# A gated cross-attention block with top-2 experts on one core: routing products in the tokens' layout, b2's products in one contraction, block-diagonal values laid out contiguously

## The reference

```python
x = x + tanh(g_xattn) * attn(layernorm(x), ctx, ctx, mask, Wq, Wk, Wv, Wo, 16)
x = x + tanh(g_ffn) * ffn(layernorm(x), Wg, bg, W1, b1, W2, b2)

# attn: 16 heads of 64
scores = einsum('bhqd,bhkd->bhqk', qh, kh) + attn_mask
ctx = einsum('bhqk,bhkd->bhqd', softmax(scores), vh)        # then Wo

# ffn: 8 experts, hidden width 256
probs = softmax(xf @ Wg + bg)
w, idx = top_k(probs, 2);  w = w / sum(w)
comb = sum(one_hot(idx, 8) * w[..., None], axis=1)
h = relu(einsum('nd,edh->enh', xf, W1) + b1[:, None, :])
y = einsum('enh,ehd->end', h, W2) + b2[:, None, :]
out = einsum('end,ne->nd', y, comb)
```

## Time and profile before

| | us |
|---|---|
| median of 3 runs | 1108.44 (1108.04 to 1109.18) |
| the profiled execution, its own time | 1107.66 |
| its span | 1105.6 |
| PE busy | 1024.9 (93%) |
| ACT busy | 943.1 (85%) |
| DVE busy | 894.4 (81%) |
| POOL busy | 791.7 (72%) |

### The profile page before, as it was taken

One profiled execution on the slowest core, in us unless ns is written; L12 is line 12 of the kernel. 1 busy time (PEld: TensorE's weight loads), 2 busy tenths in 40 slices (PEclk: granted clock), 3 DMA queues, 4 the chain that ended last, 5 costly groups with the idle time before them and its releaser, 6 DMA issues.

```text
span 1105.6 us, 36301 instructions
## 1 busy us (share of the span) xinstructions
PE 1024.9 (93%) x13797; PEld 755.4 (68%) x13797; DVE 894.4 (81%) x1803; ACT 943.1 (85%) x1809; POOL 791.7 (72%) x719
## 2 busy tenths in 40 slices
PE   5868799999999999999999999999999999999887
PEld 4446567776777777677777767777776777777655
DVE  2686688897888889788888978888897888787766
ACT  3988788889898888989888898988889898887865
POOL 3566667776867777686777768777776877788843
PEclk9999899999999999999999999999999999999999
DMA  9122121212112121211212121121212111111100
GB/s 219 33 56 59 49 56 43 55 45 59 50 40 57 52 57 43 59 50 40 57 52 56 43 59 50 40 57 52 54 45 59 50 31 46 44 40 50 29 3 20
DMA packets 123162, 56.90 MB, mean 51 GB/s; under 512 B 26584, under 2 KB 122864, under 8 KB 122992
## 3 DMA queue, kind: packets, MB, share of 16 engines
q1 hardware_dynamic: 122992, 54.59, 19.3%
HBM read 16.80 MB, written 4.19 MB: 19 GB/s over the span
## 4 chain that ended last, share of the span: by engine, by line
PE 49%; DVE 14%; ACT 12%; issue 12%; POOL 11%; DMA 1%; ACTq 0%; DVEq 0%; SPq 0%; POOLq 0%
PE bank L44 15%; PE bank L46 14%; PE bank L45 14%; POOL hidL L895 3%; POOL ptL L932 3%; ACT qH L464 3%; POOL rstd L880 3%; PE bank L307 2%; ACT bank L520 2%; PE bank L262 2%; DVE shift L668 2%; ACT x2hat L508 1%; DVE comb L868 1%; ACT vH L559 1%; DVE above L844 1%
## 5 line engine op out<-in xcount | busy, mean ns | idle before, releaser
L895 POOL TENSOR_TENSOR hidL<-hid,hidH 128x512 f16<-128x512 f32 x242 | 278.6, 1164 | 21.3 <-ACT hidH L494 21.3
L932 POOL TENSOR_TENSOR ptL<-pt,ptH 128x512 f16<-128x512 f32 x128 | 148.5, 1160 | 179.4 <-ACT pt L579 179.4
L675 DVE TENSOR_TENSOR qL<-bank,qH 128x512 f16<-128x512 f32 x224 | 153.4, 685 | 57.1 <-ACT qH L464 53.7
L484 ACT ACTIVATE hid<-bank,b1col 128x512 f32<-128x512 f32 x256 | 185.6, 725 | 8.3 <-PE bank L46 8.2
L494 ACT ACTIVATE hidH<-bank,b1col 128x512 f16<-128x512 f32 x256 | 188.3, 736 | 0.0
L464 ACT ACTIVATE qH<-bank 128x512 f16<-128x512 f32 x256 | 155.1, 609 | 36.0 <-PE bank L46 35.0
L44 PE MATMUL bank<-w2H,hidH 128*128 128x128 f16 x1024 | 179.0, 220 | 5.8 <-DVE hidL L788 5.2
L46 PE MATMUL bank<-w2H,hidL 128*128 128x128 f16 x1024 | 179.1, 220 | 0.0
L45 PE MATMUL bank<-w2L,hidH 128*128 128x128 f16 x1024 | 179.1, 220 | 0.0
L927 POOL TENSOR_TENSOR x<-x,y_scaled 128x512 f32<-128x512 f32 x114 | 146.0, 1280 | 14.1 <-DVE x L746 14.1
L938 POOL TENSOR_TENSOR prob<-prob,row_inv 128x512 f32<-128x512 f32 x128 | 133.4, 1043 | 15.2 <-DVE row_inv L782 15.2
(11 more groups left out here) (143 smaller groups left out, 3607.3 us busy)
## 6 DMA issues: line engine op xcount, KB each, us to landing
vdH<-vH SPq DMA_DIRECT2D x256, 64.0 KB, 2.1
vdL<-vL SPq DMA_DIRECT2D x256, 64.0 KB, 2.1
x_raw<-in_x SPq DMA_DIRECT2D x16, 256.0 KB, 3.0
ctx_raw<-in_ctx SPq DMA_DIRECT2D x16, 256.0 KB, 3.1
mask_raw<-in_fside_Bx1xSxS SPq DMA_DIRECT2D x32, 128.0 KB, 2.8
out_x<-x SPq DMA_DIRECT2D x16, 256.0 KB, 2.5
qH<-in_L_xattn_Wq SPq DMA_DIRECT2D x1, 512.0 KB, 6.0
qH<-in_L_xattn_Wk SPq DMA_DIRECT2D x1, 512.0 KB, 8.1
```

What stands on the lines that cost most here:

```text
L484: act.activation(hid[:, k % NR, :], bk("hid", g, e, c)[:, :], ACT.Relu, bias=b1col[:, e, c:c + 1]).then_inc(s_relu[c], 1)
L675: dve.tensor_tensor(qL[at], bk("Q", g, h)[:, :].rearrange("p (b q) -> p b q", b=GB), qH[at], ALU.subtract).then_inc(s_q_low[h % 2], 1)
L895: pool.tensor_tensor(hidL[:, m % 2, c, :], hid[:, k % NR, :], hidH[:, m % 2, c, :], ALU.subtract).then_inc(s_hid_low[c], 1)
L932: pool.tensor_tensor(ptL[:, b % 2, :], pt[:, b % 2, :], ptH[:, b % 2, :], ALU.subtract).then_inc(s_pt_low, 1)
```

## The change

Three edits.

1. The layouts of `wv`, `v` and `vd` have the chunk outside and the 64 head dimensions innermost. The 128 weights of a product lie next to each other. A placement transfer moves eight runs of 64 elements (128 B) per partition. The split of Wv at the start writes its low half in two instructions instead of one, per bank.
2. The logits are made with tokens on the partitions: the transposed activations are stationary (128 columns), `wgH`/`wgL` with 8 columns move, three passes for each of four tiles, at `i` = 0. `logitT`, `logit_t` and their transposes go, with one turn of the banks. The scale 1/32 moves into DVE's addition of the bias.
3. The three products of b2 are stacked on the partitions in blocks of 32 (`QUAD`): the weights of the picked experts are written three times (`weight3`), one transpose brings the three copies to partitions 0, 32 and 64, ACT writes all of them rounded to fp16, and DVE replaces the third by its low half. b2 is loaded three times, and its second copy replaced by its low half. One matmul per tile over 96 partitions gives the sum of the three products. The unused rows are zeroed by POOL at the start.

```diff
-CL = 4
+CW = 4
 HC = HID // P
 WS = 32.0
+QUAD = 32
+STACK = 3 * QUAD
...
-        wvH, wvL = (sb(f"wv{p}", [P, 2, C // CL, DV, CL], F16) for p in "HL")
+        wvH, wvL = (sb(f"wv{p}", [P, 2, C, DV], F16) for p in "HL")
...
-        b2H, b2L = (sb(f"b2{p}", [E, D], F16) for p in "HL")
+        b2_halves = sb("b2_halves", [STACK, D], F16)
...
-        vH, vL = (sb(f"v{p}", [P, 2, C // CL, DV, CL], F16) for p in "HL")
-        vdH, vdL = (sb(f"vd{p}", [P, 2, 2, C // CL, 2, DV, CL], F16) for p in "HL")
+        vH, vL = (sb(f"v{p}", [P, 2, C, DV], F16) for p in "HL")
+        vdH, vdL = (sb(f"vd{p}", [P, 2, 2, C, 2, DV], F16) for p in "HL")
         otH, otL = (sb(f"ot{p}", [P, 2, C, 2, S], F16) for p in "HL")
 
-        logit_t = sb("logit_t", [E, N])
...
+        weight3 = sb("weight3", [P, GT, 3, QUAD])
...
-        pickedT_H, pickedT_L = (sb(f"pickedT_{p}", [E, N], F16) for p in "HL")
+        pickedT = sb("pickedT", [STACK, N], F16)
...
-                    lhs = [v[:, t % 2, b % 2, c // CL, :, :, c % CL].rearrange("p g d -> p (g d)") for v in (vdH, vdL)]
+                    lhs = [v[:, t % 2, b % 2, c, :, :].rearrange("p g d -> p (g d)") for v in (vdH, vdL)]
...
-                if i == 7 and within(g - 1, GROUPS):
-                    for freed in take_bank("logitT", g - 1):
-                        pe.wait_ge(*freed)
-                    pe.wait_ge(s_x2T_low, g)
-                    three_passes(pe, bk("logitT", g - 1)[0:E, :], (wgH[:, :], wgL[:, :]),
-                                 (x2tH[:, (g - 1) % 2, :], x2tL[:, (g - 1) % 2, :])).then_inc(s_logitT, 1)
                 if i == 0 and within(g - 2, GROUPS):
                     for freed in take_bank("logit", g - 2):
                         pe.wait_ge(*freed)
-                    pe.wait_ge(s_logitT_out, g - 1)
+                    pe.wait_ge(s_x2T_low, g - 1)
                     for t in range(GT):
-                        last = pe.transpose(bk("logit", g - 2)[:, t * E:(t + 1) * E], logit_t[:, t * P:(t + 1) * P],
-                                            ident[0:E, 0:E])
+                        lhs = [c[:, g % 2, t * P:(t + 1) * P] for c in (x2tH, x2tL)]
+                        last = three_passes(pe, bk("logit", g - 2)[:, t * E:(t + 1) * E], lhs, (wgH[:, :], wgL[:, :]))
                     last.then_inc(s_logit, 1)
                 if i == 2 and within(g - 2, GROUPS):
                     for freed in take_bank("pickedT", g - 2):
                         pe.wait_ge(*freed)
                     pe.wait_ge(s_comb1, g - 1)
                     for t in range(GT):
-                        last = pe.transpose(bk("pickedT", g - 2)[0:E, t * P:(t + 1) * P], picked[:, t, :], ident[:, :])
+                        last = pe.transpose(bk("pickedT", g - 2)[0:STACK, t * P:(t + 1) * P],
+                                            weight3[:, t, :, :].rearrange("p n e -> p (n e)"), ident[:, :])
                     last.then_inc(s_pickT, 1)
                 if i == 3 and within(g - 2, GROUPS):
                     for freed in take_bank("b2 out", g - 2):
@@ -445,8 +442,8 @@
                     pe.wait_ge(s_pickT_low, g - 1)
                     for t in range(GT):
                         cols = slice(t * P, (t + 1) * P)
-                        last = three_passes(pe, bk("b2 out", g - 2)[:, t * D:(t + 1) * D],
-                                            (pickedT_H[:, cols], pickedT_L[:, cols]), (b2H[:, :], b2L[:, :]))
+                        last = pe.matmul(bk("b2 out", g - 2)[:, t * D:(t + 1) * D], pickedT[:, cols], b2_halves[:, :],
+                                         start=True, stop=True)
                     last.then_inc(s_b2, 1)
...
-            act.wait_ge(s_load["b2"], 16)
-            act.activation(b2H[:, :], b2_raw, ACT.Copy, scale=WS).then_inc(s_wact, 1)
+            act.wait_ge(s_load["b2"], 16 * 3)
+            act.activation(b2_halves[:, :], b2_raw, ACT.Copy, scale=WS).then_inc(s_wact, 1)
...
-                if i == 7 and within(g - 1, GROUPS):
-                    act.wait_ge(s_logitT, g)
-                    if g >= 2:
-                        act.wait_ge(s_logit, g - 1)
-                    act.activation(logit_t[:, :], bk("logitT", g - 1)[0:E, :], ACT.Copy,
-                                   scale=1.0 / WS).then_inc(s_logitT_out, 1)
...
-                weights_low(H // 4 + n, wvL[:, :, n, :, :],
-                            bk("weights", H // 4 + n)[:, :].rearrange("p (c g d) -> p g d c", c=CL, g=2), wvH[:, :, n, :, :])
+                dve.wait_ge(s_wact, H // 4 + n + 1)
+                some = slice(CW * n, CW * (n + 1))
+                for g2 in range(2):
+                    last = dve.scalar_tensor_tensor(
+                        wvL[:, g2, some, :], bk("weights", H // 4 + n)[:, :].rearrange("p (c g d) -> p g c d", c=CW, g=2)[:, g2],
+                        WS, wvH[:, g2, some, :], ALU.mult, ALU.subtract)
+                last.then_inc(s_wdve, 1)
...
-            weights_low(H // 4 + 5, b2L[:, :], b2_raw, b2H[:, :])
+            weights_low(H // 4 + 5, b2_halves[QUAD:QUAD + E, :], b2_raw[QUAD:QUAD + E], b2_halves[QUAD:QUAD + E, :])
...
-                    dve.tensor_tensor(l, bk("logit", g - 2)[:, 0:GT * E].rearrange("p (t e) -> p t e", t=GT),
-                                      bgrow[:, :].unsqueeze(1).to_broadcast([P, GT, E]), ALU.add).then_inc(s_logit_in, 1)
+                    dve.scalar_tensor_tensor(l, bk("logit", g - 2)[:, 0:GT * E].rearrange("p (t e) -> p t e", t=GT),
+                                             1.0 / WS, bgrow[:, :].unsqueeze(1).to_broadcast([P, GT, E]), ALU.mult,
+                                             ALU.add).then_inc(s_logit_in, 1)
...
-                    dve.tensor_tensor(picked[:, :, :], picked[:, :, :],
-                                      picked_inv[:, :].unsqueeze(2).to_broadcast([P, GT, E]), ALU.mult).then_inc(s_comb1, 1)
+                    if g == 2:
+                        dve.wait_ge(s_w3zero, 1)
+                    dve.tensor_tensor(weight3[:, :, :, 0:E], picked[:, :, :].unsqueeze(2).to_broadcast([P, GT, 3, E]),
+                                      picked_inv[:, :].unsqueeze(2).unsqueeze(3).to_broadcast([P, GT, 3, E]),
+                                      ALU.mult).then_inc(s_comb1, 1)
                     dve.wait_ge(s_comb1, g - 1)
                     if g >= 4:
                         dve.wait_ge(s_scaled, E * (g - 3))
-                    dve.tensor_scalar(comb[:, g % 2], picked[:, :, :], out_scale[:, 1:2], None, ALU.mult).then_inc(s_comb, 1)
+                    dve.tensor_scalar(comb[:, g % 2], weight3[:, :, 0, 0:E], out_scale[:, 1:2], None,
+                                      ALU.mult).then_inc(s_comb, 1)
                 if i == 2 and within(g - 2, GROUPS):
                     dve.wait_ge(s_pickT_high, g - 1)
-                    dve.scalar_tensor_tensor(pickedT_L[:, :], bk("pickedT", g - 2)[0:E, :], WS, pickedT_H[:, :], ALU.mult,
-                                             ALU.subtract).then_inc(s_pickT_low, 1)
+                    third = slice(2 * QUAD, 2 * QUAD + E)
+                    dve.scalar_tensor_tensor(pickedT[third, :], bk("pickedT", g - 2)[third, :], WS, pickedT[third, :],
+                                             ALU.mult, ALU.subtract).then_inc(s_pickT_low, 1)
...
-            pool.memset(vdH[:, :, :, :, :, :, :], 0.0).then_inc(s_vzero, 1)
-            pool.memset(vdL[:, :, :, :, :, :, :], 0.0).then_inc(s_vzero, 1)
+            pool.memset(b2_raw, 0.0).then_inc(s_b2zero, 1)
+            pool.memset(weight3[:, :, :, :], 0.0).then_inc(s_w3zero, 1)
+            pool.memset(vdH[:, :, :, :, :, :], 0.0).then_inc(s_vzero, 1)
+            pool.memset(vdL[:, :, :, :, :, :], 0.0).then_inc(s_vzero, 1)
...
-            load("b2", b2_raw, b2)
+            sp.wait_ge(s_b2zero, 1)
+            for n in range(3):
+                load("b2", b2_raw[n * QUAD:n * QUAD + E], b2)
...
-                            sp.dma_start(dst[g2 * S:(g2 + 1) * S, t % 2, b2_, :, g2].rearrange("p a d c -> p a (d c)"),
-                                         src[b2_ * S:(b2_ + 1) * S, g2].rearrange("p a d c -> p a (d c)")
-                                         ).then_inc(s_place[t % 2][g2], 16)
+                            sp.dma_start(dst[g2 * S:(g2 + 1) * S, t % 2, b2_, :, g2, :],
+                                         src[b2_ * S:(b2_ + 1) * S, g2]).then_inc(s_place[t % 2][g2], 16)
```

More of the change, by code:

```diff
@@ L126, in flamingo_block @@
         wg_raw = q_bytes[1][:, 2176:2176 + E]
-        b2_raw = q_bytes[1][0:E, 2304:2304 + D]
+        b2_raw = q_bytes[1][0:STACK, 2304:2304 + D]
         w1_raw = [as_f32(h[:, :, :, :], "p a c n -> p (a c n)") for h in (hidH, hidL)]
@@ L147, in flamingo_block @@
         s_q, s_v, s_scores, s_pt, s_pv, s_wo = (sem(n) for n in ("q", "v", "scores", "pt", "pv", "wo"))
-        s_hid, s_y, s_logitT, s_logit, s_pickT, s_b2 = (
-            sem(n) for n in ("hid", "y", "logitT", "logit", "pickedT", "b2out"))
```

(27 more changed lines are left out.)

## The result

The changed kernel takes 1081.91 us (1080.65 to 1082.70) against 1108.81 us, 0.9757 of the time with a 95% interval of 0.9740 to 0.9774: 26.9 us faster. The forecast was 1084.7, which is 23.7 us faster by its sum, in a range of 1077 to 1097. The profiled execution took 1082.21 us, its span 1080.4.

What follows compares the result with a forecast made beforehand. PE's issue spacing was taken as the bound. Savings of 1.57 us per group over 13.5 groups (21.2), plus 3.0 at the ramps, less 0.5 at the start, gave 23.7 us: 1084.7 us, range 1077 to 1097.

Steps and rivals of the forecast that it cites:

- What bounds the kernel: Steady part: PE issues almost without a hole and sets the pace, busy 62.45 of 64.70 us per group.
- Part 1: Value blocks: contiguous vd loads at 98 ns, not 117, saving 0.097 us per block, 12.4 us of PE time.
- Part 2: Routing products at steps 7 and 0: net 0.73 us of PE time saved per group, 11.7 us for 16.
- Part 3: b2's block: twelve matmuls become four, saving 0.45 us per group, 7.2 us in all; no price for height.
- Part 4: Placement DMAs: 128 B packets at 18 ns, 2.3 us per step, hidden behind 12 us of slack.
- rival 4: Placement DMAs: a 128 B write costs 57 ns, twice a 512 B packet, and DMA sets the pace; 1133, chance 0.08.
- What reaches the end: Of 1.96 us saved per group, 1.57 counts: routing, b2 and four value blocks; the rest falls into PE's waits.
- groups of 63.1 us: Steady part: the length of a group of eight steps expected in the profile after, where it was 64.7 us.
- The start's loss of 0.5 us: Kernel start: POOL memsets, two more b2 loads and split wvL subtractions, counted as 0.5 us lost.
- Rival 2: Steady part: other engines take over, ACT bounds more than two stretches per group, half the gain goes; 1096, chance 0.12.

Runs made afterwards that it cites:

- e3: The kernel before with b2's stacked product alone: 1098.66 us, ratio 0.9914.
- e2: The kernel before with the routing products in the tokens' layout alone: 1096.12 us, ratio 0.9892.
- e5: The kernel before with value chunks interleaved by two in place of four, vd's weights two elements apart: 1103.80 us, ratio 0.9954.
- e6: The kernel before with value chunks interleaved by eight in place of four, vd's weights eight elements apart: 1149.90 us, ratio 1.0367.
- e10: The changed kernel with each of b2's four 96-row matmuls issued three times into the same place, twelve as before: 1088.87 us.
- e1: The kernel before with the contiguous value layout and its 128 B placement runs alone: 1104.04 us, ratio 0.9962.
- e8: The changed kernel with DVE's residual ahead of y_scaled in even steps and the second layernorm's variance and root a step earlier: 1046.91 us, ratio 0.9450.

## Why the prediction was right

**What bounds the kernel.** Right: PE's spacing. What shortened it in an open stretch arrived: 0.60 of b2's 0.64 us per group (e3), and all of what was removed at step 7 (e2).

**Part 1.** Right in cause and size: 98 ns, 0.70 us. e5 and e6 settle the cause: of what the value block reads only the step changed, and the loads followed. The Trainium skill, page Advanced Engine Details and Errata, section SBUF Cachelines, asks for two hits on a 16-byte line; at 8 bytes there are two, and the load still takes 117 ns. One hit (16 bytes) is far worse, 167 ns, and four hits are free. So the rule gives the direction and is a factor of two too generous here.

**Part 2.** The mechanism was right, the term mis-sized: 0.95 us per group where I had 0.73. I had the matmuls at 29 ns (25 measured) and kept b2's handovers of 0.15 us (0.06 measured). Those belonged to the small tile (shown for b2 by e10) and went with it.

**Part 3.** Right in mechanism, mis-sized for the same reason: 0.64 in place of 0.45 (e10).

**Part 4.** Right: hidden. I took 18 ns per packet, 11 were measured, and the DMA share became 27% in a group and not near 40. The Trainium skill, page DMA: Bandwidth & Descriptors, section Specifications, has a read-modify-write below 512 B. Whether it takes place no row shows; a packet of 128 B took 11 ns against 28 for 512 B, dearer by the byte but far from the 57 ns of rival 4.

**What reaches the end.** Here two errors of opposite sign met, so that the forecast came as near as 3 us is in part luck. The sizes were too small: 37.8 us on PE, not 31.3, because the tile handovers of parts 2 and 3 were not seen as a cost of their own. And too much was taken to arrive. With the measured sizes the prediction's own count gives 0.95 + 0.64 + 4 x 0.097 = 1.98 us per group and some 30 us in all; the group lost 1.77 (64.47 to 62.70), and 26.9 us arrived. (The groups of 63.1 us that it expected are counted from 64.7; from 64.5 its sum gives 62.9.)

The missing 0.2 us per group is the saving of step 0, of the routing (0.12) and of one value block (0.10). The prediction has PE without a wait from the second layernorm's transposes to the logits, and lets the next stretch begin at the logits. The trace has DVE's `above` end 0.28 us after POOL's hidL, however early the logits are (e1, e2), so both savings came back ahead of step 1's first hidden product. The starts close the account for the changed kernel. Of the 2.37 us, 0.24 came back as a longer wait ahead of that product, 0.12 ahead of step 2's, 0.17 ahead of step 6's, and 0.10 at qL in step 6, which is the 0.6 that did not arrive. The wait for qL, the residual's in step 2 and the layernorm's chain were placed right.

The start's loss of 0.5 us has no run that shows it by itself.

**Rival 2**, ACT taking over, didn't come: ACT is busy 56.6 of 62.7 us, and PE's list of waits in the group has no entry for ACT.

## What to carry to other kernels

A PE saving is worth what lies between two waits of PE: mark them in order of time, and count each saving in its own stretch. The same layout was worth 0.26 us per group here and 0.41 after two waits had been removed. Look for waits in the distances between starts too, since a list of idle times can leave them out. And where a saving lets a chain start earlier, check that its first instruction does not simply take longer, as DVE's `above` did. When a saving arrives at 70%, look at what the remaining waits name: a residual written one place too late on DVE and a reciprocal root taken one step too late on POOL were worth 35 us (e8), more than the change itself. For a tile that uses few rows or columns of the array, look at the starts before and after its block, not only at its own spacing.

## What the runs showed of the hardware

- The stationary operand's load, fp16, 128 by 128: 98 ns at steps of 1 and 2 elements, 117 at 4, 167 at 8. Matmuls of 64 columns behind such loads start 29, 29, 33 and 60 ns apart.
- A block of matmuls on a tile of 8 rows among full ones costs 0.09 us more at each end; over 96 rows nothing (0.92 against 0.73 us for twelve).
- Matmuls of 8 moving columns with a 128-column load each start 25 ns apart.
- DMA packets of 128 B between two places in SBUF take 11 ns of an engine's time, 512 B ones 28 ns; twice as many of them change neither landing time nor the steady part.
- DVE's comparison `above` (128x256) takes 0.42 us when POOL's hidL ends 0.07 us after its start, and 0.98 to 1.13 us when hidL runs on; it then ends 0.28 us after hidL in every run looked at. What holds it was not tested.
